# A gated SmoothQuant block with a top-1 mixture of experts: turned weights, a merged logit pass, bf16 slot products and new instruction orders

## The reference

```python
# block 1: x = x + tanh(g_xattn) * f(layernorm(x)), for each of 4 batches
def _smooth_quant_linear(x, w):
    s = sqrt(max(amax_x, EPS) / max(amax_w, EPS)); s = max(s, EPS)   # per column
    xs = x / s; ws = w * s
    x_scale = max(max|xs| per row, EPS) / 127;  w_scale = the same for ws
    x_q = clip(round(xs / x_scale), -127, 127); w_q = the same for ws
    return x_q @ w_q.T * x_scale * w_scale.T
h = _smooth_quant_linear(xe, guw)            # 256x256 tokens, 256 outputs
gate, up = split(h); a = silu(gate) * up
return _smooth_quant_linear(a, dw)           # back to 256 columns

# block 2: x = x + tanh(g_ffn) * moe(layernorm(x)), 1024 tokens, 8 experts
logits = x @ w_gate; gates = softmax(logits); idx1 = argmax(gates)
locations1 = cumsum(one_hot(idx1)) - one_hot(idx1)
mask1 = one_hot(idx1) * (locations1 < 128)   # 128 slots for each expert
h = gelu(dispatched @ w1)                    # 8 x (128 x 256 x 1024)
expert_out = h @ w2                          # 8 x (128 x 1024 x 256)
combined = einsum(combine_weights, expert_out)
```

## Time and profile before

| what | value |
|---|---|
| median of 3 runs | 115.48 us (115.22 to 115.84) |
| the profiled execution | 115.32 us |
| its span | 113.6 us |
| instructions | 2268 |
| PE busy | 100.7 us, 89% |
| DVE busy | 85.1 us, 75% |
| ACT busy | 72.8 us, 64% |
| POOL busy | 55.9 us, 49% |
| DMA | 22.67 MB, mean 200 GB/s |

### The profile page before, as it was taken

One profiled execution on the slowest core, in us unless ns is written; L12 is line 12 of the kernel. 1 busy time (PEld: TensorE's weight loads), 2 busy tenths in 40 slices (PEclk: granted clock), 3 DMA queues, 4 the chain that ended last, 5 costly groups with the idle time before them and its releaser, 6 DMA issues.

```text
span 113.6 us, 2268 instructions
## 1 busy us (share of the span) xinstructions
PE 100.7 (89%) x748; PEld 85.2 (75%) x748; DVE 85.1 (75%) x254; ACT 72.8 (64%) x159; POOL 55.9 (49%) x116
## 2 busy tenths in 40 slices
PE   0997979697999979998999999999999999999910
PEld 0265649485766857894989999998999999898800
DVE  1599999989996998956647089997976759396330
ACT  5064998899999897514453798483956848494000
POOL 7065698567999678848776000522310405040131
PEclk9999999999999999999999999999999999999999
DMA  4999899898548121401388898999998100001011
GB/s 35 344 345 239 341 359 357 250 405 274 208 80 295 61 97 43 172 0 45 100 277 291 297 342 308 347 409 337 410 388 289 45 0 20 32 3 46 0 46 46
DMA packets 14091, 22.67 MB, mean 200 GB/s; under 512 B 1287, under 2 KB 11527, under 8 KB 13056
## 3 DMA queue, kind: packets, MB, share of 16 engines
q1 hardware_dynamic: 13312, 20.46, 53.1%
q0 software_dynamic: 768, 2.07, 5.6%
HBM read 20.46 MB, written 2.10 MB: 199 GB/s over the span
## 4 chain that ended last, share of the span: by engine, by line
PE 57%; DVE 22%; DMA 8%; ACT 4%; issue 3%; POOL 2%; POOLq 1%; SPq 1%; DVEq 0%
PE bk L1386 22%; PE bk L1397 13%; PE bk L1399 7%; DMA gr<-out,gidx 5%; DVE am L754 4%; DMA cw<-in_ctx_gu 3%; DVE am L717 2%; PE bk L1306 2%; PE bk L1332 2%; DVE am L710 2%; DVE wide_a L775 2%; PE bk L1362 1%; DVE ra L741 1%; PE bk L1372 1%; DVE q1s L762 1%
## 5 line engine op out<-in xcount | busy, mean ns | idle before, releaser
L467 POOL DMA_INDIRECT out<-xrow,sidx x8 | 10.9, 1357 | 38.6 <-DVE xrow L1001 38.6
L1397 PE MATMUL bk<-w2p,hh 128*128 128x512 f32 x64 | 23.4, 405 | 0.2 <-DVE hl L989 0.2
L1386 PE MATMUL bk<-rows_w,w_sb 128*128 128x128 f32 x192 | 23.2, 275 | 0.2 <-DVE rows_w L950 0.2
L1386 PEld LDWEIGHTS bk<-rows_w,w_sb 128*128 128x128 f32 x192 | 22.3, 192 | 0.9 <-DVE rows_w L950 0.6
L1399 PE MATMUL bk<-w2p,hl 128*128 128x256 f32 x64 | 17.9, 280 | 0.0
L982 DVE TENSOR_TENSOR w2p<-w_sb,w2p 128x1024 fp32r<-128x1024 f32 x12 | 14.2, 1220 | 3.5 <-ACT w2p L560 3.3
L560 ACT ACTIVATE w2p<-w_sb 128x1024 fp32r<-128x1024 f32 x12 | 12.2, 1056 | 4.9 <-PE bk L1399 4.9
L574 ACT ACTIVATE bk<-bk 128x512 f32<-128x512 f32 x16 | 9.3, 583 | 8.8 <-PE bk L1386 8.8
L989 DVE TENSOR_TENSOR hl<-bk,hh 128x512 fp32r<-128x512 f32 x16 | 10.7, 686 | 4.9 <-ACT hh L581 4.9
L1397 PEld LDWEIGHTS bk<-w2p,hh 128*128 128x128 f32 x64 | 12.0, 188 | 2.8 <-issue 0.3
L1192 PE MATMUL bk<-identb,upper 128*128 128x512 bf16 x28 | 9.8, 459 | 2.7 <-POOL upper L300 2.7
(11 more groups left out here) (164 smaller groups left out, 230.3 us busy)
## 6 DMA issues: line engine op xcount, KB each, us to landing
w_sb<-in_w SPq DMA_DIRECT2D x12, 1024.0 KB, 6.1
x<-in_x SPq DMA_DIRECT2D x4, 256.0 KB, 3.8
cw<-in_ctx_gu SPq DMA_DIRECT2D x4, 256.0 KB, 5.5
cw<-in_w SPq DMA_DIRECT2D x1, 1024.0 KB, 5.5
out<-x SPq DMA_DIRECT2D x4, 256.0 KB, 2.1
x<-in_w SPq DMA_DIRECT2D x1, 1024.0 KB
wide_a<-in_w SPq DMA_DIRECT2D x1, 1024.0 KB, 6.8
wide_b<-in_w SPq DMA_DIRECT2D x1, 1024.0 KB, 9.0
```

Of the source, the lines that this page charges most:

```text
L467: nc.gpsimd.indirect_dma_start(out_rows, bass.IndirectOffsetOnAxis(ap=sidx[:, e:e + 1], axis=0), yo[:, e % 2, :], None, bounds_check=B * T ...
L1386: ins = nc.tensor.matmul(HB[e % 2][:, m, n * C:(n + 1) * C], wv[:, k, f:f + P], xgT[:, e % B, k], start=(k == 0), stop=(k == K - 1))
L1397: nc.tensor.matmul(YB[e % 2], hh[:, e % 2, n], w2p[:, e % 2, n].rearrange("p a d -> p (a d)"), start=(n == 0), stop=False)
```

## The change

The host turns the gate and up weights and the down weights, so that they come in with the columns on the partitions. turn_w and down_turn are gone; amax_w, scale1(b, 1) and scale2 read the loaded tiles, and the four batches' damax, dguard, drecip and dfloor become one instruction each. norm1(0) moves from ScalarE to VectorE; norm1 on VectorE and POOL uses (x - mean) * rstd. ratio1 is two instructions of which each covers both columns (product_w is the new one). x and x1 get nine more columns (x1 eleven): POOL writes x's part of the logits behind x (row_part), add_x makes sum and logits in one pass, logit_rows is gone, and rsd lies behind the logits, so that sort brings expert 0's scales along. Token numbers, the layernorm's scales and the gates are split into bf16 pieces that sum to them (two, three and three); index, scales and slot_gates are bf16 matmuls; scales runs once for all batches; POOL makes the pieces in scale_pieces ahead of the gather; the sums are taken by tensor_reduce. hotc is bf16. All fills but the first six are gone. The orders of POOL, ScalarE, VectorE and TensorE are new up to expert 1; from expert 3 on they are as before. The rows of x and of the output now have gaps in SBUF, and the packets for them are 1 KB.

The diff, cut to its core:

```diff
-            sp.wait_ge(tw_ready, B)
+            sp.wait_ge(scaled1[1], B)
             load_w2(3)
...
+            def row_part(b):
+                pool.wait_ge(row1_moved, b + 1)
+                link(nc.gpsimd.tensor_tensor(std1[:, b], ve1[:, b], rs1[:, b], ALU.mult))
+                nc.gpsimd.tensor_tensor(x[:, b, :, D:D + G], xrow[:, b, T:T + J * G].rearrange("p (j g) -> p j g", g=G),
+                                        std1[:, b].unsqueeze(2).to_broadcast([P, J, G]), ALU.mult).then_inc(row_x_ready, 1)
...
+            def scale_pieces():
+                pool.wait_ge(shift2_ready, B)
+                link(nc.gpsimd.tensor_copy(rs_p[:, :, :, 0], rsd))
+                link(nc.gpsimd.tensor_tensor(rs_a[:, :, :, 0], rsd, rs_p[:, :, :, 0], ALU.subtract))
+                link(nc.gpsimd.tensor_copy(rs_p[:, :, :, 1], rs_a[:, :, :, 0]))
+                nc.gpsimd.tensor_tensor(rs_p[:, :, :, 2], rs_a[:, :, :, 0], rs_p[:, :, :, 1],
+                                        ALU.subtract).then_inc(pieces_ready, 1)
...
+            def norm1(b):
+                dve.wait_ge(rstd1_ready, b + 1)
+                for j in range(J):
+                    last = nc.vector.tensor_scalar(xn[:, b, j], x[:, b, j, 0:D], mv1[:, b, j, 0:1], rs1[:, b, j:j + 1],
+                                                   ALU.subtract, ALU.mult)
+                last.then_inc(xn_dve_ready, 1)
...
+            def damax():
+                dve.wait_ge(dw_here, 16)
+                done["damax"] = mark(nc.vector.tensor_reduce(amd[:], dw[:], AX, ALU.max, apply_absolute_value=True))
...
+                    ins = nc.vector.scalar_tensor_tensor(out=x1[:, b, j, 0:D + G], in0=bk[b][:, j, 0:D + G],
+                                                         scalar=q2g[:, b, j:j + 1], in1=x[:, b, j], op0=ALU.mult,
+                                                         op1=ALU.add)
...
             def sort(b):
                 pe.wait_ge(hot0_ready, b + 1)
-                pe.wait_ge(x1_ready, b + 1)
+                pe.wait_ge(shift2_ready, b + 1)
...
+            def scales():
+                pe.wait_ge(carried_ready, 1)
+                for n in range(B * J):
+                    ins = nc.tensor.matmul(RS, hotc[:, n // J, n % J], carried[:, n].rearrange("p a e -> p (a e)"),
+                                           start=(n == 0), stop=(n == B * J - 1))
```

More of the change, by code:

```diff
@@ L641, in _ @@
             half_logits()
+            split_high(0, 1)
             gelu_table()
+            split_high(1, 0)
             gelu(0, 0)
@@ L647, in _ @@
             hidden_high(0, 1)
+            turned(2)
             gelu(1, 0)
-            turned(2)
             gelu(1, 1)
             hidden_high(1, 0)
-            split_high(1, 0)
+            split_high(1, 1)
             hidden_high(1, 1)
-            split_high(1, 1)
             for e in range(2, E):
@@ L691, in bn @@
                 for j in range(J):
-                    done["bn", b, j] = mark(nc.vector.bn_stats(st1[:, b, j], x[:, b, j]))
+                    done["bn", b, j] = mark(nc.vector.bn_stats(st1[:, b, j], x[:, b, j, 0:D]))
             def aggr(b):
@@ L707, in amax_w @@
             def amax_w(b):
-                dve.wait_ge(tw_ready, b + 1)
-                done["amax_w", b] = mark(nc.vector.tensor_reduce(
-                    am1[:, b, K:2 * K], bk[b][:, 1, :].rearrange("p (k t) -> p k t", k=K), AX, ALU.max,
-                    apply_absolute_value=True))
+                dve.wait_ge(cw_here[b], 16)
+                done["amax_w", b] = mark(nc.vector.tensor_reduce(am1[:, b, K:2 * K], cw[:, b], AX, ALU.max,
+                                                                 apply_absolute_value=True))
             def amax_x(b):
@@ L1109, in _ @@
             pmax_(0)
-            add_x(0)
             amax4(3)
@@ L1158, in _ @@
             first_turned()
-            split_low(0, 0)
             split_low(0, 1)
+            slot_scales()
             expert_in(1)
             hidden_low(0, 0)
+            split_low(1, 0)
+            softmax()
+            expert_in(2)
             hidden_low(0, 1)
-            expert_in(2)
-            softmax()
-            expert_in(3)
-            split_low(1, 0)
+            hidden_low(1, 0)
             split_low(1, 1)
             slot_gates_out()
-            hidden_low(1, 0)
             hidden_low(1, 1)
+            expert_in(3)
             expert_add(0)
@@ L1220, in turn2 @@
                 pe.wait_ge(scaled1[a], b + 1)
+                if a == 1 and b == B - 1:
+                    pe.wait_ge(wgc_ready, 1)
                 for j in range(J):
@@ L1341, in index @@
                 for j in range(J):
-                    ins = nc.tensor.matmul(IDX, hotc[:, b, j], tokens[:, b, j], start=(b == 0 and j == 0),
-                                           stop=(b == B - 1 and j == J - 1))
+                    for h in range(1 if b == 0 else 2):
+                        ins = nc.tensor.matmul(IDX, hotc[:, b, j], tokens[:, b, j, h], start=(b == 0 and j == 0),
+                                               stop=(b == B - 1 and j == J - 1 and h == 1))
                 ins.then_inc(index_ready, 1)
-            def scales(b):
-                pe.wait_ge(hotc_ready, b + 1)
-                pe.wait_ge(carried_ready, b + 1)
-                if b == 0:
-                    pe.wait_ge(x1_ready, 2)
-                    pe.wait_ge(lg_ready, 2)
-                for j in range(J):
-                    ins = nc.tensor.matmul(RS, hotc[:, b, j], carried[:, b, j].rearrange("p a e -> p (a e)"),
-                                           start=(b == 0 and j == 0), stop=(b == B - 1 and j == J - 1))
+            def scales():
[3 more added lines that the diff above has]
+                                           start=(n == 0), stop=(n == B * J - 1))
                 ins.then_inc(slots_ready, 1)
@@ L1481, in _ @@
             hidden(1, 0)
+            hidden(1, 1)
             slots_turn(2)
-            hidden(1, 1)
             expert_out(0, 1)
```

509 lines of the change are left out of this document (229 added, 280 removed).

## The result

The changed kernel takes 123.94 us (median of 4, 123.18 to 124.44), the kernel before, beside it, 115.66 (median of 4, 115.22 to 122.54): ratio 1.072 with an interval of 1.064 to 1.081. Slower, as forecast as the likeliest sign, but by 8 us, where 116.1 was said and 118.0 was the end of the range. Some executions of nearly every kernel here, the kernel before included, are over 1.5% longer than its fastest; they are called slow and the others fast, and every ratio compares fast ones alone. The profiled execution took 124.27 us.

A forecast was written before the change was run, and what follows sets the result against it. The prediction took VectorE and ScalarE, both almost full, to bound the front, and TensorE the part from 57.59 us on. Its sum was 115.32 - 1.0 (front) + 0.3 (to expert stage) + 1.5 (first experts) = 116.1 us, range 113.9 to 118.0.

The forecast's parts named there:

- its term of 0.7 us: Front: transposes early on at 1.2 GHz once the fills are gone, VectorE waiting for them: +0.7 us, bounds 0 to 3.
- the risk of this change: Removing the fills could let TensorE's clock fall, early and around 51 us; the sum counted it early alone.
- rival D: Clock stays at 1.2 GHz through turns and products of batches 0 and 1: +3 us, 118.4 us, chance 0.12.
- T: The mark the forecast counts from: the end of add_x(3), 46.55 us in the kernel before.
- The front's work: Up to the end of add_x(3): less busy time on VectorE, 1.7 us gained, limited by ScalarE's 1.9 us idle.
- The early part of the clock: turn_x(0) to turn_x(2) and some turn2 still at 1.2 GHz, 0.52 us more each.
- The worry that more_consts would take the gain back: Front: six short POOL operations moved into the rounds could reduce the 1.7 us gain by as much.
- T to the expert stage: From the end of add_x(3) through pieces, index, gather and sorts: +0.3 us, bounds -0.5 to +1.0.
- The first experts: Cheaper slot gates, but TensorE idles 2.6 us at slots_turn(3) waiting for expert_in(3): +1.5 us net.
- B: No wait at slots_turn(3) because VectorE is ready: 113.4 us, faster, chance 0.12.
- C: Front gains 3 to 3.5 us from VectorE's saved work and idle time: 113.7 to 114.1 us, chance 0.15.
- E: Clock rises early and the front gains 1.7 us: 115.4 us, no visible change, chance 0.16.

The follow-up runs named there:

- the run without the middle fills: Best version (changed kernel plus fills, early expert_in(3), POOL's multiply-and-add, nine early fills) without its ten fills between 30 and 42 us: 116.12 us.
- after: The changed kernel as it stands, against the kernel before: 123.94 us, ratio 1.072.
- after + fills + expert_in(3): Changed kernel with 32 fills put back at TensorE's waits and expert_in(3) moved forward behind hidden_low(0, 1) on VectorE: 114.02 us (fast median), ratio 0.988.
- the early fills: Nine fills between turn_x(0) and turn2(0, 1), added to the changed kernel with fills, early expert_in(3) and POOL's multiply-and-add: 112.89 us, ratio 0.977.
- the kernel before with expert_in(3) late: Kernel before, all fills kept, with expert_in(3) moved on VectorE from behind softmax() to behind hidden_low(1, 1): 121.14 us (fast median), ratio 1.052.

## Why the prediction was right or wrong

**The step that failed** is the clock: "my sum has it early alone, since later gaps are under 1 us", and its term of 0.7 us. Both halves of the reason were wrong. Later gaps were longer: 2.70 us ahead of turn_x(3), 1.33 at 44.51, 2.18 at slots_turn(3), the last of which my own sum contained. And gaps under 1 us were enough where TensorE had little work: at 35 us in the changed kernel, and in the run without the middle fills. I had called the removal of the fills "the risk of this change" and gave its mechanism to rival D, at 118.4 us and a chance of 0.12, but ended D at batches 0 and 1 for no reason that a row gave. In place of 0.7 us the clock costs 52.58 - 46.47 = 6.1 us up to T (after against after + fills + expert_in(3)), and about 1.8 more behind slots_turn(3). Put back, the fills alone bring 5.4 us; in the kernel before, taking them out costs 3.1 by the fastest run and 5.4 by the median.

**The front's work.** Forecast -1.7, with ScalarE's idle time as the limit. The change as it stands has -0.08 at full clock: a second term was missing, POOL's subtraction, an edit of form (it saves shift1(3)) that I had not costed at all, taking the instruction at its old duration. Without it and with the early fills it is -1.15, in the range of 1 to 1.9 for half to all of that time only just. ScalarE is then nearest to full, but its idle time between 11.44 and 39.46 us fell only from 1.91 to 1.57 us, so that it is the limit isn't shown. The early part of the clock came as said: turn_x(0) took 1.12 us, and turn_x(1) and (2) 2.16 together, against 0.66 each at full clock; its price by itself wasn't measured. The maximum over 1024 elements took 1.21 (1.2). The worry that more_consts would take the gain back was the wrong way round. At T the sum is: 6.1 for 0.7 of clock and -0.1 for -1.7 of work, together the 7 us by which T was missed.

**T to the expert stage.** The index came at T + 3.1 (3.5 forecast), the pieces were done at 56.53 + 0.22, T + 4.2 (4.1), the gather started at T + 4.9 (4.6 to 5.1). expert_out(0, 0) began at 63.45, T + 10.9, against T + 11.0 before (57.59 us): -0.1 instead of +0.3, in its bounds.

**The first experts.** The wait is where it was put, released by the operation that was named, for the reason given (queue order on VectorE): 2.2 us for 2.6. From hidden(1, 0) to slots_turn(3) 75.02 - 65.08 = 9.94 us, forecast 10.1 (which is 1.4 over the 8.67 of before, and not the 1.5 of the sum). The slot gates take 0.35 us for 1.69. What was missing is what the wait does to the clock: at 76 to 80 us it is 0.57, and such a rate over 4 us costs 0.43 x 4 = 1.7. From slots_turn(3) to the end it is 122.5 - 75.02 = 47.5 us, before 113.6 - 67.89 = 45.7: 1.8 more, the term that I had at nothing. Moving one line takes wait and low clock away together, 3.5 to 4.9 us; in the kernel before nearly the same wait costs 5.8.

**The signs.** Rival D's sign, transposes of over 1 us after 16 us, is there: 1.12 us at 19.32. So the view that I named would have told it, and the mechanism was in my hands; its extent was guessed. But D's time, 118.4, was 5.5 too low. Rivals B, C and E are out.

**What stays open.** Why one run of ten without the middle fills kept the clock; how much each place of the fills is worth by itself, but for the ten ahead of turn_x(3); how the granted clock's mean goes with the time, since the four executions of after have means of 0.909, 0.979, 0.888 and 0.947 at 124.27, 123.62, 123.18 and 124.44 us; and what rows of 1 KB cost, which wasn't tried by itself (VectorE's first operation on x starts at 4.06 us, 4.12 before; the 256 KB of x1 land 2.6 us from issue, 2.1 before).

## What to carry to other kernels

A matmul that fills a gap may be dear to remove, although it computes nothing and hides under other engines: before taking fills out, go through the timeline for each wait of TensorE and each thin stretch, at either clock, and price the stretch behind it at 1.2 GHz. Price a wait put on a busy TensorE as itself and that stretch, here together about twice its length, and look for the one line in another engine's order that avoids it. Where a step changes the form of an operation, its duration has to come from a row with that engine and that form, or be bounded as unknown.

## What was unexpected in the hardware

- A single gap of 2.2 to 2.5 us on a TensorE that is otherwise full is followed by a granted clock of 0.50 to 0.57 over about four microseconds (after at 76 to 80 us; the kernel before with expert_in(3) late at 72 to 76 us, where a wait of 2.46 costs 5.8 us in all).
- The same program may keep the clock or lose it: 112.73 us once at a mean clock of 0.99, 115.53 to 117.06 nine times at 0.948 to 0.965.
- On GpSimd a tensor_scalar of 128x256 f32 takes 1228 ns with the mean subtracted and 556 ns with the negated mean (which lies in another tile) added in its place.
- The granted clock of 1.00 in the first slices doesn't agree with the transposes there: four take 1.12 us at 8.78, as they do at 19.32 where the slice says 0.60. In that part the duration of a known group tells the level, the clock row doesn't.
